# Four chained layers on one core: layer 3's opening set among layer 2's last steps

## The chip, the cores and the metric

The kernel runs on one core of a Trainium2 chip. A core has five engines: TensorE (PE) multiplies matrices, VectorE (DVE) and ScalarE (ACT) work elementwise, GpSimd (POOL) does simple elementwise work and memory fills, SyncE (SP) issues transfers. Each runs its own instruction list in order and waits on counters (semaphores) that others raise. Data lie in SBUF, products land in PSUM, which has eight banks. The metric is the device time of one execution in microseconds.

## The reference, cut to what matters

```python
x: (16, 64, 16, 16) f32
x = layer 0: group norm, 1x1 convolution, a gated mixture of basis functions; added to x
x = layer 1: group norm, a state-space block with a 3x3 depthwise convolution; added to x
x = layer 2: group norm, attention of 8 heads over the 256 places of an image; added to x
x = layer 3: group norm, modulated deformable 3x3 convolution; added to x

# layer 3, for each image
n      = group_norm(x)
offset = conv3x3(n, off_w) + off_b            # 18 channels: dy and dx of 9 taps
mask   = sigmoid(conv3x3(n, mask_w) + mask_b) # 9 channels
for tap in 9:                                 # ky, kx
    py, px = row + ky - 1 + dy, col + kx - 1 + dx
    samp[tap] = bilinear(n, py, px) * mask[tap]     # zero outside the image
x += weight . samp + bias
```

The opening norm of each layer is over pairs of channels of one image. Bilinear sampling is done without gathering: the weight of source row r for position py is a "hat", max(0, 1 - |py - r|), and likewise for columns, so that a sample is a matrix product with (row hat x column hat) as weights.

## The kernel before

Two images lie on the 128 partitions (64 channels each), so there are 8 pairs and 4 groups of 4 images. `program` calls `layer0` to `layer3` in turn; each has a block of its own, between which all engines meet at a barrier.

**Layer 2** (L761 to L1109) is a software pipeline written out by hand. `ROWS` (L777) are steps v from -19 to 143, eight for each image (k = v % 8, c = v // 8), and every engine's list goes through them. At step v TensorE computes score tiles for the maxima of step v + 19 (`largest`, L1027), until v = 108; the score tile v (`scores`, L1038), until v = 127; and, at fixed k, the products of the context (`context`, L1058), its turning (`turn_context`, L1072, k = 5), turning back (`turn_back`, k = 0) and the projection (`project`, k = 3). VectorE takes maxima, divides the context (`normalize`, k = 5) and adds the result to x (`add`, L925, k = 3); ScalarE takes exponentials of every score tile. POOL splits the maxima in two halves, SP sends them (`send_maxima`, L828) into the stacks `q_st` that the scores read. The last 16 steps have no scores left, only the last images' contexts.

**Layer 3** (L1112 to L1568) first has an opening. The norm of all pairs (`GroupNorm`, L114) goes through three engines; VectorE writes the padded images `xpad` (L1300), three queues send them into `stack` (L1175); TensorE convolves offsets and masks for group 0 (`conv_offsets`, L1459: 24 products and 4 for the grid), ScalarE takes them out of PSUM (`take_offsets`, L1362). For chunk 0 (4 images) positions and masks are spread to all places by products (`spread_positions` L1468, `spread_masks` L1475), in thirds of three taps; for later chunks they go through DRAM (`load_positions`, `load_masks`). From each third come the hats (`take_distance`, `make_hat`), weighed by the mask (`weigh_hat`, L1189) and split into three bf16 parts (`take_first`, `take_rest`, `take_second`, `take_last`), on VectorE and ScalarE for chunk 0, on POOL and ScalarE for the others. SP copies the parts into `hats[b]`, b = 0 or 1 for the pair of the chunk (`send_hats`, L1230). In between, TensorE weighs pair 0 (`weigh`, L1482) and convolves groups 1 to 3.

Then comes the loop over 8 pairs n and 9 taps t (L1554), v = 9 n + t. At each tap TensorE spreads the row hats of v + 1 and the column hats of v + 2 (`spread_rows`, `spread_cols`), weighs one sixth of the next pair in taps 2 to 7, and adds the samples of v to `acc` (`samples`, L1513). VectorE multiplies row and column weights (L1335) and copies one half of the weighed images (L1311); ScalarE copies the column weights (`take_cols`) and the other half, and does one of the 12 `hat_steps` (L1416) of the next chunk at each tap: step h of the chunk at tap h of its two pairs. `spread_cols` waits for the hats in SBUF at the start of each pair (L1505); `take_first` (L1389) waits until the former chunk's hats have left `parts`.

## Time and profile before

| | |
|---|---|
| three timed runs | 524.96, 528.49, 530.88 us; median 528.49 |
| profiled execution | span 528.0 us, first to last instruction; the page gives no other time for it |
| busy in the span | PE 439.1 us (83%), weight loads 231.3, DVE 342.4 (65%), ACT 288.9 (55%), POOL 132.8 (25%) |
| layer 2, steps from the first score tile | about 218 to 348 us |
| layer 3's opening | 348 to 383.6 us |
| layer 3's loop | 383.6 to 522.8 us |

Busy means that an instruction was under way, not that the engine was at its peak. The chain of waits that ended last shows PE with 13% of the span, POOL 6%, DMA 5%, SP's queue 3%, ACT 3%, DVE 2%; PE's granted clock has two levels, 1.0 (2.4 GHz) and 0.5 (1.2 GHz), and a number between them is a mean over a stretch.

### The profile page before, as it was taken

The page shows a single profiled execution, that of the slowest core. Times are in us where ns is not written, and L with a number is a line of the kernel's source. Part 1 is how long each engine was busy: PE and PEld are TensorE (multiplying, and loading weights), DVE is VectorE, ACT ScalarE, POOL GpSimd, SP SyncE. Part 2 cuts the span into 40 slices and gives each one's busy share as a digit, 9 for nine tenths or more (in the row PEclk, how much of TensorE's full clock was granted, in tenths as well). Part 3 has the DMA queues.
Part 4 walks back from the last instruction along what each step waited for, and adds up shares of the span by engine and source line. Part 5 has one row for each costly group of instructions (what it writes and reads, how often), then busy time and mean ns, then how long its engine had stood idle before and what let it go on. Part 6 is the DMA issues. An engine that isn't in the chain of part 4 may idle for free. (4 is left out here: it accounts for less than half of the span.)

```text
span 528.0 us, 9368 instructions
## 1 busy us (share of the span) xinstructions
PE 439.1 (83%) x3406; PEld 231.3 (44%) x3406; DVE 342.4 (65%) x668; ACT 288.9 (55%) x511; POOL 132.8 (25%) x162
## 2 busy tenths in 40 slices
PE   0527768899999887679999999939898999999995
PEld 0216648555455664223333333324443454454442
DVE  4549876233344568978999996251654778777784
ACT  1279955131532437047878778722865578486441
POOL 4420004000000005744422212031364428065000
PEclk9956997999999988559999999957977999999999
DMA  5500000900000004952200000016390480933302
GB/s 142 164 0 1 0 0 1 197 1 1 0 1 0 1 0 107 279 175 67 73 27 3 3 2 4 0 47 160 100 226 15 89 181 2 217 55 68 67 2 79
DMA packets 20767, 33.79 MB, mean 64 GB/s; under 512 B 5657, under 2 KB 15497, under 8 KB 19957
## 3 DMA queue, kind: packets, MB, share of 16 engines
q1 hardware_dynamic: 16724, 23.70, 18.9%
q0 software_dynamic: 2176, 6.35, 4.3%
q10 hardware_dynamic: 1824, 3.19, 2.3%
q8 instruction: 26, 0.43, 0.4%
q14 instruction: 17, 0.13, 0.1%
HBM read 16.21 MB, written 4.64 MB: 39 GB/s over the span
## 5 line engine op out<-in xcount | busy, mean ns | idle before, releaser
L1335 DVE TENSOR_TENSOR L_s<-L_row_ps,L_cols 128x1024 f32<-128x1024 f32 x72 | 87.6, 1218 | 9.3 <-PE L_row_ps L1500 7.5
L910 DVE TENSOR_REDUCE L_mx<-L_ring 128x2 f32<-128x512 f32 x128 | 83.3, 686 | 12.4 <-PE L_ring L1034 11.8
L965 ACT ACTIVATE L_e<-L_ring 128x512 f32<-128x512 f32 x128 | 73.7, 597 | 21.4 <-PE L_ring L1047 19.3
L1523 PE MATMUL L_acc<-L_s,L_t_sb 128*64 128x256 f32 x576 | 81.6, 406 | 1.1 <-DVE L_s L1335 1.0
L1404 ACT ACTIVATE L_cols<-L_col_ps 128x512 f32<-128x512 f32 x72 | 42.8, 596 | 48.9 <-PE L_col_ps L1510 48.5
L1034 PE MATMUL L_ring<-stacks_k_st,stacks_q_st 64*128 64x256 bf16 x256 | 51.0, 301 | 7.0 <-DMA stacks_k_st<-L_k_parts 4.7
L1523 PEld LDWEIGHTS L_acc<-L_s,L_t_sb 128*64 128x64 f32 x576 | 36.0, 140 | 35.9 <-DVE L_s L1335 19.8
L1047 PE MATMUL L_ring<-stacks_q_st,stacks_k_st 64*128 64x256 bf16 x256 | 47.2, 282 | 1.2 <-DMA stacks_q_st<-L_m_parts 1.2
L1500 PE MATMUL L_row_ps<-L_hats,L_sel 48*128 48x512 bf16 x144 | 44.6, 392 | 0.0
L1067 PE MATMUL L_ctx_ps<-L_e,L_v_x 128*32 128x256 f32 x512 | 41.5, 398 | 0.0
L1311 DVE COPY L_t_sb<-L_acc 128x192 f32<-128x192 f32 x48 | 17.1, 357 | 31.4 <-PE L_acc L1491 31.4
L1034 PEld LDWEIGHTS L_ring<-stacks_k_st,stacks_q_st 64*128 64x128 bf16 x256 | 15.9, 98 | 43.8 <-DVE L_mx L910 24.2
L382 PE MATMUL L_y<-L_t,all_w_post 128*128 128x256 f32 x96 | 25.3, 418 | 11.5 <-DVE L_t L342 11.5
L1510 PE MATMUL L_col_ps<-L_hats,L_sel 48*128 48x512 bf16 x72 | 28.7, 400 | 7.0 <-DMA L_hats<-L_parts 5.0
L1491 PE MATMUL L_acc<-all_w_all,L_xn 64*128 64x192 f32 x96 | 26.8, 362 | 5.0 <-DVE L_t_sb L1311 2.7
L382 PEld LDWEIGHTS L_y<-L_t,all_w_post 128*128 128x128 f32 x96 | 19.4, 208 | 17.1 <-DVE L_t L342 14.2
L1491 PE MATMUL L_col_ps<-all_w_all,L_xn 64*128 64x192 f32 x96 | 26.7, 360 | 0.0
L853 POOL MEMSET L_v_x<- 128x1024 f32 x1 | 1.0, 951 | 101.7 <-POOLq L496 101.7
L1200 POOL TENSOR_TENSOR L_hat<-L_hat,L_mask 64x768 f32<-64x768 f32 x9 | 16.3, 1812 | 40.1 <-ACT L_hat L1382 40.1
L415 ACT ACTIVATE L_uu<-L_z,L_minus_mu,L_inv 128x256 f32 x48 | 24.4, 586 | 1.3 <-DVEq L314 1.3
L633 ACT ACTIVATE L_sq<-L_t_ps 128x1024 f32<-128x1024 f32 x4 | 4.1, 1024 | 34.9 <-PE L_t_ps L716 34.9
L656 PE MATMUL L_xs_ps<-L_stack,L_w_tap 128*128 128x512 f32 x48 | 22.7, 601 | 0.0
(270 smaller groups left out, 814.2 us busy)
## 6 DMA issues: line engine op xcount, KB each, us to landing
L_hats<-L_parts SPq DMA_DIRECT2D x28, 216.0 KB, 5.0
L_hat<-L_offsets SPq DMA_DIRECT2D x20, 192.0 KB, 4.7
L_mask<-L_offsets SPq DMA_DIRECT2D x10, 192.0 KB, 4.9
stacks_q_st<-L_q_parts SPq DMA_DIRECT2D x12, 128.0 KB, 3.9
stacks_k_st<-L_k_parts ACTq DMA_DIRECT2D x12, 128.0 KB, 4.8
stacks_q_st<-L_q_parts POOLq DMA_DIRECT2D x12, 128.0 KB, 2.7
stacks_k_st<-L_k_parts POOLq DMA_DIRECT2D x12, 128.0 KB, 2.9
L_stack<-L_xpad SPq DMA_DIRECT2D x7, 162.0 KB, 5.8
```

The lines of the kernel that those rows point to most:

```text
L382: mm = pe.matmul(y2[:, ds(k, 1), :], w_post[:], t[:, q, j:j + 1, :], start=False, stop=(j == NB - 1))
L910: dve.tensor_reduce(mx[:, n % 2, :, head], ring[:, place(step) % 3].rearrange("p (q s) -> p q s", q=2), AX.X, ALU.max).then_inc(max_read, 1)
L965: act.activation(e[:, k], ring[:, 3 + v % 3], ACT.Exp, scale=HD2 ** -0.5).then_inc(e_ready, 1)
L1034: mm = pe.matmul(ring[:, place(step) % 3, q * N:(q + 1) * N], rows_of(q_st, n, h, p)[:, q * P:(q + 1) * P], rows_of(k_st, n, h, p), start= ...
L1047: mm = pe.matmul(ring[:, 3 + v % 3, t * N:(t + 1) * N], rows_of(k_st, c, h, p)[:, t * P:(t + 1) * P], rows_of(q_st, c, h, p), start=True, ...
L1067: mm = pe.matmul(ctx_ps[32 * j:32 * j + 32, g * N:(g + 1) * N], v_x[:, c % 2, t, 4 * g + j, :], e[:, 4 * g + j, t * N:(t + 1) * N], start= ...
L1335: dve.tensor_tensor(s[:, q], row_ps[:, q], cols[:, t % 3:t % 3 + 1].broadcast_to([P, 2, 2 * N]), ALU.mult).then_inc(s_ready, 1)
L1404: act.activation(cols[:, v % 3], col_ps[:, c % 2], ACT.Copy).then_inc(col_read, 1)
L1491: mm = pe.matmul(out, xn[rows, b, k // 3 * P:(k // 3 + 1) * P], w_all[rows, k % 3 * TW:(k % 3 + 1) * TW], start=True, stop=True)
L1500: mm = pe.matmul(row_ps[:, v % 2, h], sel[0:3 * H, h], hats[0:3 * H, n % 2, :, t * N:(t + 1) * N], start=True, stop=True)
L1510: pe.matmul(col_ps[:, c % 2], sel[C:C + 3 * H, 2], hats[C:C + 3 * H, n % 2, :, t * N:(t + 1) * N], start=True, stop=True).then_inc(col_rea ...
L1523: mm = pe.matmul(acc[C * e:C * e + C, b, 0:N], t_sb[:, b, h, (KK * e + t) * C:(KK * e + t + 1) * C], s[:, q, h, e * N:(e + 1) * N], start= ...
```

## The change

Layer 3's opening gets a class of its own, `Opening`, whose methods are called from layer 2's step lists and then from layer 3. Its norm is done in two lots of four pairs; its buffers `parts`, `hats`, `s` and `cols` lie in layer 2's stacks, and the padded images stay in memory from layer 0 on (`Pads`), cleared once on POOL. In layer 2, lot 0's norm stands at steps 79 to 85, group 0's offsets at 109 to 115, chunk 0's first two thirds of hats at 116 to 134 with part of the last third, and group 1's offsets at 137 to 143. What is left for layer 3 is the end of the last third, lot 1's norm and pair 0's weighing. The offsets of groups 2 and 3 are convolved after taps (0, 8) and (1, 5) of the loop. Masks in layer 2 are made of exp and ln instead of the sigmoid table. The ScalarE hat steps of chunks 1 and 2 come two taps later. All transfers of layer 3 are issued by SP.

```diff
 # layer 2, SP
+for j in range(4):
+    send_maxima(NQ - 1, j)
+    if j < 2:
+        opening.send_group(sp, j)
+sp.wait_ge(s_ready, 8 * 12)
+sp.wait_ge(opening.parts_ready, 2)
+opening.send_hats(sp, 0, slice(0, 2 * opening.THIRD))
 # layer 2, POOL, after image n
+if n in (12, 13):
+    opening.pad_group(pool, x, n - 12)
+if n == 14:
+    opening.copy_selection(pool)
+    for p in range(2):
+        opening.normalize_pair(pool, x, p)
 # layer 2, VectorE, at the end of step v
+if v == 79:
+    dve.wait_ge(signals.x_stats, 3 * NP + 4)
+    opening.aggregate(dve, 0)
+if v == 83:
+    opening.variances(dve, 0, a_ps[:, P:P + 4])
+if v == 85:
+    opening.shifts(dve, 0)
+if v == 116:
+    opening.take_offsets(dve, 0, ring[:, 2, 0:N])
+if v in (118, 125):
+    opening.below_by_vector(dve, (v - 118) // 7, pos_ps)
+if v in (119, 126):
+    opening.hat_by_vector(dve, (v - 119) // 7, pos_ps)
+if v in (121, 128):
+    opening.weigh_hat(dve, (v - 121) // 7, mask_ps, True)
+if v == 122:
+    opening.take_first(dve, 0)
+if v == 123:
+    opening.take_rest(dve, 0)
+if v == 124:
+    opening.take_second(dve, 0)
+if v == 125:
+    opening.take_last(dve, 0)
+if v == 131:
+    opening.take_rest(dve, 1)
+if v == 133:
+    opening.take_last(dve, 1)
+if v == 134:
+    opening.weigh_hat(dve, 2, mask_ps, False)
 # layer 2, ScalarE, at the end of step v
+if v == 84:
+    opening.scales(act, 0, a_ps[:, P + 4:P + 8])
+if v == 116:
+    opening.take_masks(act, 0)
+if v == 129:
+    opening.first_by_scalar(act, 1)
+if v == 130:
+    opening.distance_by_scalar(act, 2, pos_ps)
+if v == 132:
+    opening.second_by_scalar(act, 1)
+if v == 131:
+    opening.hat_by_scalar(act, 2)
+if v == 143:
+    opening.offsets_by_scalar(act, 1, ring[:, 0, 0:N])
+    opening.take_masks(act, 1)
 # layer 2, TensorE, within step v
+if v == 83:
+    pe.wait_ge(ctx_copied, c - 1)
+    opening.means(pe, 0, a_ps[:, P:P + 4])
+if v == 84:
+    opening.spreads(pe, 0, a_ps[:, P + 4:P + 8])
+if 109 <= v < 116:
+    if v == 109:
+        pe.wait_ge(max_read, 126)
+    opening.convolve(pe, 0, ring[:, 2, 0:N], v - 109, v - 108)
+if v == 117:
+    pe.wait_ge(max_read, 8 * B)
+    pe.wait_ge(m_read, B)
+    opening.spread_positions(pe, 0, pos_ps)
+if v in (123, 130):
+    third = (v - 116) // 7
+    pe.wait_ge(opening.masked, third)
+    opening.spread_positions(pe, third, pos_ps)
+if v in (120, 127, 132):
+    third = (v - 120) // 6
+    pe.wait_ge(opening.dist_ready, third + 1)
+    if third < 2:
+        pe.wait_ge(opening.hat_ready, third + 1)
+    opening.spread_masks(pe, third, mask_ps)
+if v >= 137:
+    if v == 137:
+        pe.wait_ge(opening.dist_ready, 3)
+    opening.convolve(pe, 1, ring[:, 0, 0:N], v - 137, v - 136)
...
+class Opening:
...
+    def convolve(self, pe, g, out, first, last):
...
+        for k in range(first, last):
+            for j in range(4):
+                if k < 6:
+                    pe.matmul(out[32 * j:32 * j + 32], w_off[:, k, :], tap(self.stack, 4 * g + j, k), start=(k == 0), stop=False)
+                else:
+                    mm = pe.matmul(out[32 * j:32 * j + 32], w_grid[:], grid[:], start=False, stop=True)
...
+    def take_masks(self, act, g):
+        act.wait_ge(self.off_ready, g + 1)
+        act.activation(self.sig[:, g], self.off[:, g], ACT.Exp, scale=-1.0).then_inc(self.mask_own, 1)
+        act.wait_ge(self.mask_own, 2 * g + 1)
+        act.activation(self.sig[:, g], self.sig[:, g], ACT.Ln, bias=1.0).then_inc(self.mask_own, 1)
+        act.wait_ge(self.mask_own, 2 * g + 2)
+        act.activation(self.sig[:, g], self.sig[:, g], ACT.Exp, scale=-1.0).then_inc(self.sig_ready, 1)
...
+CONVOLVED = {(0, 8): 2, (1, 5): 3}
+MASKED = {(0, 8): (), (1, 0): (2,), (1, 7): (3,)}
 # layer 3, SP (all transfers of the layer)
+store_group(sp, 1)
+sp.wait_ge(stored[1], 32)
+load_positions(sp, 1, 0)
+load_masks(sp, 1, 0)
+sp.wait_ge(parts_ready, 3)
+sp.wait_ge(hats_in[0], 64)
+opening.send_hats(sp, 0, slice(2 * THIRD, TN))
+for g in (2, 3):
+    opening.send_group(sp, g)
+for j in (1, 2):
+    load_positions(sp, 1, j)
+    load_masks(sp, 1, j)
+opening.send_hats(sp, 1, slice(0, TN))
+store_group(sp, 2)
 # layer 3, VectorE, before the loop
+opening.aggregate(dve, 1)
+dve.wait_ge(first_ready, 2)
+for k in range(2):
+    take_first_image(0, k, k, first_ps[k])
+opening.variances(dve, 1, mean_ps)
+dve.wait_ge(first_ready, 4)
+for k in range(2, 4):
+    take_first_image(0, k, k, first_ps[k])
+opening.take_rest(dve, 2)
+for k in range(4, 6):
+    take_first_image(0, k, k, first_ps[k])
+opening.shifts(dve, 1)
+opening.take_last(dve, 2)
 # layer 3, ScalarE, in the loop
+                    late = 2 if n < 4 else 0
...
-                        h = KK * (n % 2) + t
-                        if n < NP - 2 and h < len(hat_steps):
+                        if (n, t) in CONVOLVED:
+                            g = CONVOLVED[n, t]
+                            opening.offsets_by_scalar(act, g, col_ps[:, turns.bank["conv", g], 0:N])
+                        if (n, t) == (0, 0):
+                            act.preload_act_table_set("sigmoid_and_others")
+                        h = KK * (n % 2) + t - late
+                        if n < NP - 2 and 0 <= h < len(hat_steps):
                             hat_step, j = hat_steps[h]
                             hat_step(n // 2 + 1, j)
 # layer 3, TensorE, in the loop
                         samples(n, n % 2, t)
+                        if (n, t) in CONVOLVED:
+                            g = CONVOLVED[n, t]
+                            bank_read(("conv", g))
+                            opening.convolve(pe, g, col_ps[:, turns.bank["conv", g], 0:N], 0, 7)
```

## Rows read from the trace of the kernel before

**Rows 1.** Table of stretches: us, busy us (instructions) of each engine, granted clock, DMA share, GB/s.

```profile
330.90:337.00 6.10, 5.77 (x58) 2.29 (x57) 1.09 (x4) 5.08 (x10) 0.20 (x1) 1.00 0.00 1
...
347.90:383.60 35.70, 27.19 (x282) 14.96 (x283) 15.90 (x43) 18.30 (x31) 12.69 (x20) 0.79 0.46 116
...
383.60:399.50 15.90, 13.87 (x84) 6.12 (x82) 9.54 (x11) 8.03 (x14) 7.13 (x9) 0.81 0.90 195
...
399.50:407.00 7.50, 6.84 (x30) 3.27 (x31) 2.98 (x4) 4.74 (x10) 4.17 (x3) 0.54 0.01 2
...
423.50:439.50 16.00, 16.00 (x127) 8.24 (x125) 12.92 (x17) 12.48 (x25) 5.96 (x4) 1.00 0.61 129
```

**Rows 2.** Timeline of the seam: start, us, engine, line, what; last: barrier passed.

```profile
328.87 0.39 PE L1047 MATMUL L_ring<-stacks_q_st,stacks_k_st 64*128 64x256 bf16 x2
...
329.18 0.64 PE L1067 MATMUL L_ctx_ps<-L_e,L_v_x 128*32 128x256 f32 x8
...
340.96 0.33 PE L1083 MATMUL L_a_ps<-all_ident,L_ctx_n 128*128 128x128 f32 x1
...
347.99 1.28 ACT L174 ACT_TABLE_LOAD   x1 [2.44 <-PEq L823]
```

**Rows 3.** Timeline of TensorE: positions, masks (not shown), positions, convolution, the next one.

```profile
364.76 1.56 PE L1472 MATMUL L_row_ps<-L_off,all_to_places 128*128 128x256 f32 x6
...
367.69 1.56 PE L1472 MATMUL L_row_ps<-L_off,all_to_places 128*128 128x256 f32 x6
...
370.67 2.80 PE L1463 MATMUL L_row_ps<-L_stack,all_w_off 128*32 128x256 f32 x48
...
373.71 2.77 PE L1463 MATMUL L_row_ps<-L_stack,all_w_off 128*32 128x256 f32 x48
```

**Rows 4.** Timeline of ScalarE and VectorE in the opening, and a group of the page.

```profile
364.60 0.47 ACT L1365 ACTIVATE L_sig<-L_row_ps,all_l_vec 128x256 f32<-128x256 f32 x1
...
368.16 0.68 DVE L1196 TENSOR_TENSOR L_hat<-L_hat,L_row_ps 64x512 f32<-64x512 f32 x1 [8.14 <-ACT L_hat L1382]
...
370.95 0.96 DVE L1208 TENSOR_TENSOR L_rest<-L_hat,L_parts 128x768 f32<-128x768 f32 x1 [1.78 <-ACT L_parts L1391]
...
L1311 DVE COPY L_t_sb<-L_acc 128x192 f32<-128x192 f32 x48 | 17.1, 357 | 31.4 <-PE L_acc L1491 31.4
```

**Rows 5.** Chain of waits: a transfer's issue, the landing of pair 1's hats; transfers by size.

```profile
383.07 0.59 SPq L1173
...
392.01 6.66 DMA L_hats<-L_parts
...
L_stack<-L_xpad SPq DMA_DIRECT2D x7, 162.0 KB, 5.8
```

**Rows 6.** Timeline of the loop: VectorE's first samples, then TensorE's taps.

```profile
383.64 2.36 DVE L1335 TENSOR_TENSOR L_s<-L_row_ps,L_cols 128x1024 f32<-128x1024 f32 x2 [1.31 <-ACT L_cols L1404]
...
400.16 0.60 PE L1510 MATMUL L_col_ps<-L_hats,L_sel 48*128 48x512 bf16 x1 [1.97 <-ACT L_cols L1404]
...
403.32 0.60 PE L1500 MATMUL L_row_ps<-L_hats,L_sel 48*128 48x512 bf16 x1
...
406.82 0.39 PE L1500 MATMUL L_row_ps<-L_hats,L_sel 48*128 48x512 bf16 x1
...
408.37 0.39 PE L1500 MATMUL L_row_ps<-L_hats,L_sel 48*128 48x512 bf16 x1
...
422.54 0.39 PE L1510 MATMUL L_col_ps<-L_hats,L_sel 48*128 48x512 bf16 x1 [1.08 <-DMA L_hats<-L_parts]
```

**Rows 7.** Chain of waits, and timeline of TensorE: chunk 2's third hat, its landing.

```profile
438.00 0.74 ACT L_hat L1382
...
455.81 0.39 PE L1510 MATMUL L_col_ps<-L_hats,L_sel 48*128 48x512 bf16 x1 [0.92 <-DMA L_hats<-L_parts]
```

**Rows 8.** Timeline of VectorE in layer 2: a cast alone, one beside POOL.

```profile
201.05 0.43 DVE L895 CAST L_parts<-L_e 128x512 bf16<-128x512 f32 x1
...
206.25 1.26 DVE L895 CAST L_parts<-L_e 128x512 bf16<-128x512 f32 x1
```

632 lines of the change are left out of this document (345 added, 287 removed).

## The prediction

> **What bounds the kernel now.** I read the table of stretches first, then the timeline of each engine around the seam between layers 2 and 3, then the chain of waits. In about steps 115 to 122 of layer 2 (330.9 to 337.0) TensorE is busy 5.77 of 6.10 us while VectorE does 1.09 us and POOL almost nothing; in layer 3's opening, 347.9 to 383.6, it is busy 27 of 35.7 us at a granted clock of 0.79; in a settled image pair of the sampling loop it is busy 16.00 of 16.00 us [rows 1]. So the seam costs 35.65 us from the barrier (347.99) to the first sample multiplication (383.64) [rows 2, 6], and the time is won only if the work put among layer 2's steps fits where TensorE is idle. It mostly doesn't: a score step takes 0.31 us (328.87 to 329.18) and a context step follows at once [rows 2]. TensorE is itself what bounds those steps; the idle engine there is VectorE. Only the last steps (128 to 143, from 340.96 to 347.7) have holes, because there each product waits for the one before.
>
> **The change, part by part.**
>
> *Norm of the first four pairs at steps 79 to 85.* Nine small VectorE operations and two small products. VectorE works beside a TensorE that never waits long, but the spread product waits in TensorE's order for four dependent VectorE steps. Between nothing (all hidden) and 1.5 us; I take 0.5, since the products themselves are tiny.
>
> *First offsets at steps 109 to 115.* Seven pieces of the convolution, 28 products. The same 28 took 3.04 us (370.67 to 373.71) at full clock [rows 3]. TensorE is full there, so all of it lengthens layer 2: **+3.0**.
>
> *Positions and masks at steps 117, 120, 123, 127.* One third of both took 2.93 us (364.76 to 367.69) [rows 3]. Two thirds: **+5.9**.
>
> *The wait before step 127's masks.* TensorE waits in its own order for `hat_ready`. VectorE has, since the first masks landed, to weigh the hat (0.68, then about 0.4 and 0.6 for the two smaller pieces), cast it, take the rest (0.96), cast again (0.65 each, by 0.43 for 512 columns), add an image and divide another (about 1.1), then do two operations over 768 columns out of PSUM with a subtraction of 0.96 between them [rows 4, 8]. Two PSUM multiplications of 1024 columns take 2.36 [rows 6], so 768 take about 0.9. With ten hand-overs of about 0.1 that is 8.9 us after the first masks' end, against 6.6 us of TensorE's own work (seven rows of 0.3 to 0.9, and 1.45 of positions) [rows 2, 3]. I take **+2.3**; between 0 and 5. Behind it in TensorE's order stand the contexts and everything of the tail.
>
> *The tail, steps 128 to 143.* Before, from 340.96 to the barrier at 347.99, 7.0 us [rows 2]. Now in this order: turning back and two context steps (1.4), a wait for the second weighing (0.3), positions (1.5), projection (0.6), the wait for ScalarE's distance (0.6), masks (1.45), turning image 15 (0.6), its division (0.9), turning back and two pieces of convolution (1.2), projection (0.6), the other pieces (2.1), ScalarE's offsets and three dependent operations for the mask (0.47 each, with gaps 2.1) [rows 3, 4]. With 0.3 for the barrier 13.6 us, so **+6.6**; between +3 (the holes swallow a third's products) and +9.
> Layer 2 thus ends at 347.99 + 0.5 + 3.0 + 5.9 + 2.3 + 6.6 = **366.3**.
>
> *Moved to POOL and SP.* Padding and the xn copies are POOL's at images 12 to 14, where it idles; two groups of stack transfers go between maxima, four instructions of 0.63 us each [rows 5], inside a lead of a whole image, about 7 us. Cost nothing; without that cover, two stalls of about 2 us.
>
> *What is left of the opening.* VectorE: aggregation 0.35, six copies of 0.36, five small operations with their hand-overs 1.2, the third's rest and last part 0.96 each [rows 4], and about 1.2 of waits for ScalarE and TensorE: 6.8 us, between 6 and 9. The first multiplication is at 373.1 instead of 383.64, 10.5 us earlier. The two-thirds hats were issued in layer 2's tail and are in by then.
>
> *The transfers after it.* This is what is late next. SP now issues, alone and in order: group 1's two stores and a wait for their landing (3.5 us), three loads (1.9), then waits for the third part (6.8), four hat transfers, eight stack transfers of groups 2 and 3 (of about 160 KB), six loads, and only then pair 1's four hat transfers: 22 times 0.63, so the last is issued at 6.8 + 14.0 = 20.8 us after the barrier and lands 5.0 to 6.7 later [rows 5]. The volume agrees: 3.6 MB at the 195 GB/s of the loop's first 16 us is 18 us [rows 1]. Pair 1's hats are in at 26.3 us, 392.6; before they came at 398.67 (392.01 and 6.66) [rows 5]. Tap 7 of pair 0 cannot begin before. Before it began at 403.32 [rows 6]; now at 392.7: **-10.6**. Both have a stop of about 2 us ahead of it, and before, the clock then was 0.54 over 7.5 us [rows 1]. Its price was two taps of about 3.5 (403.32 to 406.82) instead of 1.9, one of them before 403.32 [rows 6]. I take the same cost after tap 7 as before; between 1.6 cheaper and 3.3 dearer.
>
> *Offsets of groups 2 and 3 between taps.* A tap is TensorE's from end to end: 1.55 us without weighing (406.82 to 408.37) [rows 6], and (16.0 - 3 x 1.55) / 6 = 1.89 with it [rows 1]. Twice 3.04 [rows 3]: **+6.1**. VectorE has one tap in hand and covers none of it.
>
> *The hat steps two taps later.* They are tied to taps on ScalarE, and each chunk's hats must land before tap 7 of an odd pair. Chunk 1 before: TensorE stood 1.1 us until 422.54 [rows 6]. Chunk 2 before: ScalarE's third hat (438.00) began a chain over POOL, SP and the transfer that landed 17.8 us later, just before 455.81, and TensorE waited about 1 us for it [rows 7]. In the new chunk 1 that hat stands behind group 2's convolution, about 33.6 us after the barrier, so the chain ends at 51.4, where TensorE arrives at 48.7: 2.7 of waiting, **+1.6**; between 0 and 4. In the new chunk 2 the chain begins two weighed taps later (2 x 1.89) while TensorE arrives as before: **+3.8**; between 0 and that.
>
> **Sum.** -10.6 + 6.1 + 1.6 + 3.8 = +0.9 us. The page gives a span of 528.0 and no other time for that execution; it is 0.5 below the median of the three runs, 528.49 (524.96 to 530.88). So 528.49 + 0.9 = **529.4 us**: no change that can be told, 1% (5.3 us) being about what a measurement of this kernel tells from nothing.
>
> A third weighing: POOL pads groups 2 and 3 while VectorE forms the last part in the opening. The trace has such a pair: a cast of 512 columns takes 0.43 us alone and 1.26 beside POOL's subtraction [rows 8]. The Trainium skill, "SBUF — State Buffer", section Who interferes with whom, says that the two engines share one port pair, that a VectorE instruction with two SBUF inputs or in a two-port mode contends with POOL, and that whoever comes second waits the whole instruction. By that rule the third part would be late by one POOL operation, at most about 0.8 us, and the sum 530.2; by the row of 0.96 for the same subtraction it is 529.4.
>
> **Rivals.**
> *Faster: the waits are not there.* If VectorE is ahead at step 127 (-2.3), the tail grows by 3 only (-3.6) and the full clock holds after the stop (-1.6), and the late hat steps cost half (-1.9), the time is 520.0. For it: the tail's TensorE is free for half its length; my hand-overs are generous. Against it: each of the four is a sum of measured operations. Chance 0.27.
> *Slower: the clock falls in layer 2's tail.* The place is step 127, the first wait of more than 2 us in a stretch that ran at 1.00 throughout. After such a stop at 398.2 to 400.16 the granted clock was near its lower level of 1.2 GHz (0.54 in that stretch), and a row product took 0.60 us instead of 0.39 [rows 1, 6]. If it falls there, it decides the case: positions, masks and the second convolution, 1.45 + 1.45 + 3.04 and the turns between, take about 6 us more, and the opening's twelve weighings and first taps 2 more: 537. It needs the wait to reach about 2 us, which my sum has just over that line. For it: before, the seam itself ran at 0.79 [rows 1]. Against it: here there are 1.4 us products between the waits. Chance 0.21.
> The Trainium skill, "TensorE: Matmul & The Clock Gate", section HAM oscillation, says that waits between bursts throttle the array again, so that the next burst starts slow; this trace agrees at 400 us.
> *Slower: the maxima.* If a stack group's 0.65 MB holds image 14's maxima back, two stalls of 2 us: 533.3 and, with any of the above, over the line. Chance 0.05.
> *The change doesn't do what it says*, the work staying in a row because a semaphore holds it to the old order: about 529 to 535. Chance 0.02.
>
> **Chances.** The forecast's own case has 0.45, with its own range 524 to 534. Faster by over 1% (under 523.2): the first rival, 0.27. Within 1%: 0.46. Slower (over 533.8): 0.21 + 0.05 and a little: 0.27. The range of 8 in 10 runs from the faster rival's value to just beyond the clock's: 519 to 538.
>
> **What would show it.** Right: the barrier to layer 3 at about 366 and the first row-and-column multiplication at about 373; TensorE's steps 109 to 127 longer by some 11 us, with one wait of 2 to 3 us before a mask product; pair 1's hats landing 26 us after the barrier; two taps of 5 us with the convolutions in them; waits of about 2.7 and 5 us before tap 7 of pairs 1 and 3, and of about 1 before that of pair 5 as before. Wrong: a barrier before 362 or after 371; a granted clock of 0.5 in layer 2's last steps; no longer wait before tap 7 of pair 3, which would mean that the hats are not tied as I say.

## The result: slower by 2.3%, and where the profile after shows it

The changed kernel took 539.15 us (median of four runs, 537.00 to 542.91); beside it on the same chip the kernel before took 527.53 us (four runs, 524.96 to 530.88). The ratio is 1.0229, 95% interval 1.0171 to 1.0287. Ratios here come from runs side by side without the slower executions (over 1.5% above the fastest of their kernel), medians and ranges from all of them, so that the quotient of two medians can differ from the ratio by up to 0.4%. The forecast was 529.4 with a range of 519 to 538, and "within 1%" as the likeliest of three. It was wrong. The profiled execution of after took 539.36 us, its span is 537.6: 9.6 more than the span of before. The account below is made of spans.

The page of the kernel after: span, busy time, and the granted clock in 40 slices of 13.4 us.

```profile
span 537.6 us, 9381 instructions
PE 445.5 (83%) x3422; PEld 234.1 (44%) x3422; DVE 345.4 (64%) x670; ACT 284.2 (53%) x510; POOL 123.1 (23%) x147
PEclk9857988999999997579999999995859999799899
```

TensorE's busy time grew by 6.4 us with 16 more matrix instructions recorded, so most of that is slower instructions, not more of them. In the clock row the digits below 9 late in the span are slices 28 and 29 from the left counted from zero (376 to 403 us), 34 (457 to 470) and 37 (497 to 511), beside the opening's own (27). The table of stretches shows the first of them closer (us, busy us of each engine, granted clock, DMA share, GB/s):

```profile
358.00:365.00 7.00, 4.21 (x61) 2.18 (x62) 2.90 (x8) 2.00 (x5) 0.00 (x0) 0.96 0.28 89
365.00:374.00 9.00, 7.84 (x35) 5.19 (x35) 5.31 (x18) 4.58 (x12) 2.70 (x4) 0.50 0.28 95
...
384.00:394.00 10.00, 7.12 (x38) 2.79 (x34) 4.01 (x5) 3.24 (x7) 2.63 (x2) 0.72 0.85 174
394.00:404.00 10.00, 9.63 (x77) 4.36 (x80) 2.71 (x3) 2.97 (x5) 1.64 (x1) 0.60 0.00 0
```

Layer 2's barrier was passed at 364.8 us (SP's first instruction behind it; forecast 366.3) and the first sample multiplication came at 373.36 (forecast 373.1; before 383.64, [rows 6]). Up to there the change does what it should: it wins 10.3 us. Then the loop gives back 19.9. VectorE multiplies samples once per tap, so the start of that instruction is a clock on every tap, and the timelines of the two kernels give this table (starts of the sample multiplication, us):

| from tap (pair, tap) | to | before | after | more | forecast |
|---|---|---|---|---|---|
| (0,0) at 383.64, 373.36 | (0,8) | 21.66 | 22.40 | +0.7 | -0.1 |
| (0,8) | (1,3) | 7.41 | 13.48 | +6.1 | +3.05 |
| (1,3) | (1,7) | 7.51 | 11.14 | +3.6 | +3.05 |
| (1,7) | (2,1) | 6.22 | 7.36 | +1.1 | +1.6 |
| (3,7) | (4,2) | 7.60 | 14.12 | +6.5 | +3.8 |
| (5,7) | (6,1) | 6.18 | 7.94 | +1.8 | 0 |

All other taps are equal to 0.02 us. The sum (before rounding) is +19.9, less 10.3 is +9.6, the whole difference of the spans. The three rows that were missed most are the three in which a stop of TensorE is followed by slow instructions. First, the timeline around the end of pair 0 (start, us, engine, line, what, and in brackets the idle time before and who ended it):

```profile
387.09 0.94 ACT L1634 ACTIVATE L3o_shared<-L3o_shared,all_l_vec 128x768 f32<-128x768 f32 x1 [3.02 <-DMA L_mask<-L_masks]
...
388.56 0.60 PE L1754 MATMUL L_col_ps<-stacks_q_st,L3o_sel 48*128 48x512 bf16 x1 [1.63 <-ACT stacks_q_st L1661]
...
394.37 0.60 PE L1754 MATMUL L_col_ps<-stacks_q_st,L3o_sel 48*128 48x512 bf16 x1 [1.62 <-DMA stacks_q_st<-stacks_k_st]
...
400.32 3.64 PE L1331 MATMUL L_col_ps<-stacks_stack,all_w_off 128*32 128x256 f32 x48
...
404.52 0.47 ACT L1345 ACTIVATE L3o_off<-L_col_ps,all_l_vec 128x256 f32<-128x256 f32 x1 [5.37 <-PE L_col_ps L1333]
404.89 0.83 ACT L1640 ACTIVATE L3o_shared<-L3o_shared 128x768 f32<-128x768 f32 x1
```

ScalarE stands 3.0 us for chunk 1's loads, with TensorE behind it; then TensorE stands for pair 1's hats until 394.4. A column product takes 0.60 us where it takes 0.39 at full clock, and group 2's convolution takes 3.64 us against 2.80 [rows 3]: the granted clock is 0.50 from 400.3 to 402.0 and 0.99 behind that. ScalarE waited 5.37 us for it, and its hat (404.89) stood behind. SP's queue says why both transfers were late:

```profile
373.22 2.49 SPq L1439 DMA_DIRECT2D stacks_q_st<-stacks_k_st  x4
375.76 0.65 SPq L1310 DMA_DIRECT2D stacks_stack<-stacks_xpad  x1
...
380.38 0.61 SPq L1311 DMA_DIRECT2D stacks_stack<-stacks_xpad  x1
381.03 1.25 SPq L1509 DMA_DIRECT2D L3o_shared<-L_offsets  x2
...
385.57 2.77 SPq L1439 DMA_DIRECT2D stacks_q_st<-stacks_k_st  x4
```

Eight stack transfers that nobody needs before tap 8 stand ahead of the loads (tap 4 to 7) and of the hats (tap 7). Second, TensorE's timeline before tap 7 of pair 3 and behind it, with the stretch it lies in:

```profile
455.59 0.60 PE L1743 MATMUL L_row_ps<-stacks_q_st,L3o_sel 48*128 48x512 bf16 x2
...
460.94 0.61 PE L1754 MATMUL L_col_ps<-stacks_q_st,L3o_sel 48*128 48x512 bf16 x1 [4.75 <-DMA stacks_q_st<-stacks_k_st]
...
462.12 1.97 PE L1767 MATMUL L_acc<-stacks_k_st,L_t_sb 128*64 128x256 f32 x8
...
464.03 0.60 PE L1743 MATMUL L_row_ps<-stacks_q_st,L3o_sel 48*128 48x512 bf16 x1
```
```profile
460.00:466.00 6.00, 5.06 (x22) 2.27 (x24) 2.39 (x3) 1.80 (x4) 0.00 (x0) 0.51 1.04 264
466.00:472.00 6.00, 6.00 (x45) 2.54 (x43) 4.14 (x6) 4.30 (x8) 1.48 (x1) 0.92 0.89 165
```

The stop was 0.92 us before [rows 7] and is 4.75 now: 3.83 more, the forecast to 0.03. What was not forecast is the line at 462.12: the samples of a tap take 1.97 us instead of 1.08, two taps run at the lower clock (1.2 GHz), and 2.7 us more are gone. In four experiments with this stop left as it is, (3,7) to (4,2) took 12.9 to 13.2 us instead of 14.1, so the part behind the stop is 1.4 to 2.7 us, by the execution.

The other rows vary by execution too. The row from (1,7) has a stop of 2.19 us behind which the clock stayed up:

```profile
423.85 0.39 PE L1754 MATMUL L_col_ps<-stacks_q_st,L3o_sel 48*128 48x512 bf16 x1 [2.19 <-DMA stacks_q_st<-stacks_k_st]
...
424.49 1.08 PE L1767 MATMUL L_acc<-stacks_k_st,L_t_sb 128*64 128x256 f32 x8
```

In five experiments that leave this place alone (chunk 2 on time, step 127, both fills, the convolution two taps later) the stop is 2.0 to 2.3 us, the clock fell at it each time, and the row took 8.7 to 10.4 us instead of 7.4. The row from (0,8) took 11.4 to 12.5 us in four experiments that leave it alone, instead of 13.5. In the one whose loop is wholly unchanged (step 127) the loop from first to last sample multiplication took 154.8 us, here 156.2, before 136.3: the whole differs by 1.4 us, the row from (3,7) alone by 1.3 and the one from (1,7) by 1.6 the other way.

### The profile page after: what moved, and what is told of

The parts are those of the page before. It is cut to its first block and busy times, and to the rows that moved or that the text cites. A ratio compares the mean times of both kernels' runs of the same rounds, so it can differ in the third digit from the quotient of the medians.

```text
span 537.6 us, 9381 instructions
## 1 busy us (share of the span) xinstructions
PE 445.5 (83%) x3422; PEld 234.1 (44%) x3422; DVE 345.4 (64%) x670; ACT 284.2 (53%) x510; POOL 123.1 (23%) x147
## 3 DMA queue, kind: packets, MB, share of 16 engines
q1 hardware_dynamic: 18608, 25.70, 19.3%
## 5 line engine op out<-in xcount | busy, mean ns | idle before, releaser
L1609 DVE TENSOR_TENSOR stacks_k_st<-L_row_ps,stacks_q_st 128x1024 f32<-128x1024 f32 x72 | 87.6, 1218 | 17.5 <-PE L_row_ps L1743 17.0
L932 DVE TENSOR_REDUCE L_mx<-L_ring 128x2 f32<-128x512 f32 x128 | 83.4, 686 | 10.9 <-PE L_ring L1101 10.2
L1767 PE MATMUL L_acc<-stacks_k_st,L_t_sb 128*64 128x256 f32 x576 | 84.6, 418 | 0.9 <-DVE stacks_k_st L1609 0.8
L1661 ACT ACTIVATE stacks_q_st<-L_col_ps 128x512 f32<-128x512 f32 x72 | 42.9, 596 | 55.0 <-PE L_col_ps L1754 54.8
L1767 PEld LDWEIGHTS L_acc<-stacks_k_st,L_t_sb 128*64 128x64 f32 x576 | 37.1, 144 | 38.5 <-DVE stacks_k_st L1609 18.1
L1743 PE MATMUL L_row_ps<-stacks_q_st,L3o_sel 48*128 48x512 bf16 x144 | 46.2, 404 | 0.1
L1754 PE MATMUL L_col_ps<-stacks_q_st,L3o_sel 48*128 48x512 bf16 x72 | 30.0, 416 | 12.6 <-DMA stacks_q_st<-stacks_k_st 9.9
L383 PE MATMUL L_y<-L_t,all_w_post 128*128 128x256 f32 x96 | 25.0, 415 | 11.7 <-DVE L_t L343 11.7
L1557 POOL TENSOR_TENSOR L3o_shared<-L3o_shared,L_mask 64x768 f32<-64x768 f32 x9 | 16.3, 1816 | 65.1 <-ACT L3o_shared L1640 65.1
L1734 PE MATMUL L_col_ps<-all_w_all,L3o_xn 64*128 64x192 f32 x92 | 25.4, 363 | 0.0
L1734 PE MATMUL L_acc<-all_w_all,L3o_xn 64*128 64x192 f32 x88 | 23.9, 356 | 0.6 <-ACT stacks_q_st L1661 0.3
L663 PE MATMUL L_xs_ps<-stacks_stack,L_w_tap 128*128 128x512 f32 x48 | 22.7, 601 | 0.0
```

Source lines behind the costliest of these rows:

```text
L383: mm = pe.matmul(y2[:, ds(k, 1), :], w_post[:], t[:, q, j:j + 1, :], start=False, stop=(j == NB - 1))
L932: dve.tensor_reduce(mx[:, n % 2, :, head], ring[:, place(step) % 3].rearrange("p (q s) -> p q s", q=2), AX.X, ALU.max).then_inc(max_read, 1)
L1609: dve.tensor_tensor(s[:, q], row_ps[:, q], cols[:, t % 3:t % 3 + 1].broadcast_to([P, 2, 2 * N]), ALU.mult).then_inc(s_ready, 1)
L1661: act.activation(cols[:, v % 3], col_ps[:, turns.bank["cols", v]], ACT.Copy).then_inc(col_read, 1)
L1734: mm = pe.matmul(out[e], xn[rows, b, k // 3 * P:(k // 3 + 1) * P], w_all[rows, k % 3 * TW:(k % 3 + 1) * TW], start=True, stop=True)
L1743: mm = pe.matmul(row_ps[:, v % 2, h], sel[0:3 * H, h], hats[0:3 * H, n % 2, :, t * N:(t + 1) * N], start=True, stop=True)
```

## The experiments

Each time is compared with runs of the kernel before that were taken beside it on the same chip. "At (p,t)" is tap t of pair p.

### Chunk 2's hat steps on time

```diff
-                    late = 2 if n < 4 else 0
+                    late = 2 if n < 2 else 0
```

> Only chunk 2's hat steps go back to their old taps (two taps earlier); chunk 1's stay late. Theory A (the delay of the hat steps is what makes the stop before tap 7 of pair 3, and the stop is what drops the clock): the stop falls from 4.75 us to about 1, no tap after it runs at the lower clock, and between the sample multiplications of (3,7) and (3,8) lie 3.1 to 3.6 us instead of 7.4. That gives back 6.5 us: about 532.7 us, ratio to the kernel before 1.010. Theory B (the chain is late because POOL and SP still work on chunk 1 and on group 3's stores): the chain ends as late as now, the stop stays over 4 us, ratio 1.02.

534.08 us (531.71 to 541.50), ratio 1.0116, interval 1.0060 to 1.0171: about 1.1% under the change as it is. Theory A holds as to the time. The profiled execution is itself the longest of the five (541.5 us), so its clock is not typical of them. In it the stop before tap 7 of pair 3 is 2.15 us, and the clock then stays low until past 470 us.

```profile
460.99 0.39 PE L1754 MATMUL L_col_ps<-stacks_q_st,L3o_sel 48*128 48x512 bf16 x1 [2.15 <-DMA stacks_q_st<-stacks_k_st]
```
```profile
460.00:466.00 6.00, 5.01 (x27) 1.93 (x27) 2.71 (x3) 1.90 (x4) 0.00 (x0) 0.72 1.04 251
466.00:472.00 6.00, 6.00 (x27) 2.32 (x25) 2.84 (x3) 2.75 (x4) 1.11 (x1) 0.50 0.70 124
```

The stop is not back at 0.92 us, and that is no matter of this execution: in the profiles of the three later experiments with the same steps on time and the same loads behind the hats it is 2.17 or 2.18 us. The two taps are 2.6 of the 3.83 us. The other 1.2 lie in the transfers: from SP's first issue of the hats to TensorE's use of them it is 6.9 us in the kernel before and 8.15 here (452.84 to 460.99):

```profile
448.89 2.66 SPq L1236 DMA_DIRECT2D L_hats<-L_parts  x4
```
```profile
452.84 2.67 SPq L1439 DMA_DIRECT2D stacks_q_st<-stacks_k_st  x4
```

### Pair 1's hats ahead of the stacks

```diff
                 opening.send_hats(sp, 0, slice(2 * THIRD, TN))
-                for g in (2, 3):
-                    opening.send_group(sp, g)
-                for j in (1, 2):
-                    load_positions(sp, 1, j)
-                    load_masks(sp, 1, j)
+                load_positions(sp, 1, 1)
+                load_masks(sp, 1, 1)
                 opening.send_hats(sp, 1, slice(0, TN))
+                load_positions(sp, 1, 2)
+                load_masks(sp, 1, 2)
+                for g in (2, 3):
+                    opening.send_group(sp, g)
```

> SP's order after the third hats is changed alone: loads of chunk 1's second third, pair 1's four hats, loads of the last third, and only then the eight stack transfers of groups 2 and 3. Theory A (SP's order of issue sets both stops of pair 0: ScalarE's 3.0 us wait for the loads at 387.1 and TensorE's wait for pair 1's hats until 394.4): pair 1's hats are in at about 386, TensorE never stops 1.5 us in pair 0, the granted clock stays at 1.00, taps 7 and 8 take 1.9 instead of 5.6 and 2.8 us, and group 2's convolution 3.1 instead of 6.4 less 1.55. Some 3 + 2 + 1.9 + 0.9 = 7 to 9 us less: about 531, ratio 1.007; the later waits (1,7) and (3,7) may take 1 to 2 of it back, since chunk 1's chain then meets a TensorE that arrives sooner. Theory B (the transfers are bound by volume, not by order): the hats land at 391 or later, and the stacks then hold up the convolution; ratio 1.02.

531.47 us (531.00 to 532.86), ratio 1.0092, interval 1.0061 to 1.0123. Theory A. The clock is full after pair 0's first taps, and from (0,6) to (1,1) it takes 9.8 us instead of 19.3:

```profile
384.00:394.00 10.00, 9.97 (x80) 5.36 (x79) 8.31 (x11) 8.30 (x16) 5.28 (x3) 1.00 1.04 216
394.00:404.00 10.00, 9.65 (x104) 4.61 (x104) 4.83 (x7) 6.32 (x12) 5.15 (x4) 1.00 0.10 32
```

Some comes back at once, but not by the way that was expected. TensorE arrives 7 us sooner and (1,7) to (2,1) takes 10.2 us instead of 7.4, yet the stop in it is 2.28 us against 2.19: the hats moved along with the taps. What is new is the lower clock behind the stop, which the profile of the kernel after does not have there:

```profile
416.91 0.60 PE L1755 MATMUL L_col_ps<-stacks_q_st,L3o_sel 48*128 48x512 bf16 x1 [2.28 <-DMA stacks_q_st<-stacks_k_st]
...
418.08 1.97 PE L1768 MATMUL L_acc<-stacks_k_st,L_t_sb 128*64 128x256 f32 x8
```

From (0,8) to (1,3), with the same convolution and the full clock, it takes 10.4 us; the forecast had 10.5 (7.41 and 3.05), the profile after 13.5.

### Both together

The two edits above.

> Both edits together. If the two losses are separate places, the gains add: 539.2 - 6.5 - 7.5 = 525, ratio 0.996, within half a per cent of the kernel before. If the clock or one chain links them, the sum is smaller: ratio 1.005 to 1.01.

527.54 us (522.03 to 534.62, ten runs), ratio 0.9966, interval 0.9924 to 1.0009. The gains add: 1.0116 and 1.0092 are 0.0113 and 0.0137 under 1.0229, and 0.9966 is 0.0263 under it. The runs scatter over 12.6 us, with stops of 2.2 us left in the profile.

### Without the late convolutions

This kernel leaves out the 24 products over the stacks in each of the two convolutions; the last argument lets the four grid products start the sum.

```diff
...
-                            opening.convolve(pe, g, col_ps[...], 0, 7)
+                            opening.convolve(pe, g, col_ps[...], 6, 7, True)
```

> Left out: the 24 products over the stacks in the convolutions of groups 2 and 3; only the four grid products of each remain, so the offsets of images 8 to 15 are wrong. All waits, stores, loads and transfers stay. Theory A (the convolutions cost their own time on TensorE, more for group 2 since it runs at the lower clock): 3.6 us at the lower clock and 2.6 at full clock go, 6 us in all, and what hangs behind group 2 (ScalarE's third hat of chunk 1 at 404.9) comes 3.6 us earlier too, so no wait before tap 7 of pair 1 grows: 532 to 533 us, ratio 1.010. Theory B (the hat chain, not TensorE, sets the end of each two pairs): TensorE arrives earlier and waits longer before (1,7) and (3,7), and less than 3 us is gained, ratio 1.017.

536.90 us (534.93 to 540.52), ratio 1.0215, interval 1.0160 to 1.0269; span 533.1, 4.5 under the change. So B is nearer: (0,8) to (1,7) takes 5.6 us less, but (1,7) to (2,1) takes 11.7 us instead of 7.4. Of these 4.3 us, 1.6 are the stop (3.77 us instead of 2.19), because the hats of chunk 1 do not come sooner by as much; the other 2.7 are slow taps, since here the clock fell at that stop (0.50 from 418.8 to 425.6) and in the profile after it did not. How much of the convolutions' own time a chain of hats takes back, one execution of each does not tell.

### Everything early

```diff
-                load_positions(sp, 1, 0)
-                load_masks(sp, 1, 0)
+                for j in range(3):
+                    load_positions(sp, 1, j)
+                    load_masks(sp, 1, j)
                 sp.wait_ge(parts_ready, 3)
                 sp.wait_ge(hats_in[0], 64)
                 opening.send_hats(sp, 0, slice(2 * THIRD, TN))
+                opening.send_hats(sp, 1, slice(0, TN))
                 for g in (2, 3):
                     opening.send_group(sp, g)
-                for j in (1, 2):
-                    load_positions(sp, 1, j)
-                    load_masks(sp, 1, j)
-                opening.send_hats(sp, 1, slice(0, TN))
...
-                    late = 2 if n < 4 else 0
+                    late = 1 if n < 2 else 0
```

> SP issues all of chunk 1's loads ahead of its wait for the third part (it idles from 368.9 to 373.2 there), then the third hats, pair 1's hats, and the stack transfers last; chunk 1's hat steps stand one tap late instead of two, chunk 2's on time. Theory A (what is left in the run with both first edits is chunk 1's chain: 3.0 us of waiting before tap 7 of pair 1 and 1.7 of slow taps behind it): the wait goes, (1,7) to (1,8) takes 1.9 us instead of 4.5, and the whole is 4 us under that run: 523.5 us, ratio to the kernel before 0.989. Theory B (POOL's nine operations of a chunk, about 15.5 us, set the end whatever the taps): the wait shrinks by less than 1 us and the ratio stays 0.996.

524.96 us (522.96 to 529.07, ten runs), ratio 0.9972, interval 0.9936 to 1.0007. Between A and B: (1,7) to (1,8) takes 2.9 us (4.5 with both edits, 1.9 without a wait), and (1,7) to (2,1) 5.8 instead of 9.0; of these 3.2 us, 1.6 are the stop (0.66 us instead of 2.25) and the rest is the clock, which fell at the longer one. The median is 2.6 lower than with both edits, the ratio is not: against ten scattered runs the difference can't be told. The stop before tap 7 of pair 3 is 2.18 us, and the clock fell behind it (0.50 from 448.9 to 452.3).

### Step 127 of layer 2

```diff
 # VectorE
-                    if v == 125:
+                    if v == 126:
                         opening.take_last(dve, 0)
 # TensorE
-                    if v in (120, 127, 132):
+                    if v in (120, 132):
...
+                    if v == 129:
+                        pe.wait_ge(opening.hat_ready, 2)
+                        opening.spread_masks(pe, 1, mask_ps)
```

> Only layer 2's step 127 is changed: VectorE takes the first third's last part after the second third's hat instead of before it (0.93 us), and TensorE's second mask products stand at step 129, behind one context step (0.42 us). Theory A (the 2.32 us stop and the lower clock in the masks behind it, 2.79 us instead of 1.5, come from this order): the stop falls to about 1.0, the masks take 1.5, the layer's barrier comes 2 to 2.6 us earlier, about 537, ratio 1.018. Theory B (the tail is bound by another chain, VectorE to ScalarE to TensorE for the last third and images 14 and 15): the barrier moves by less than 0.7 us, ratio 1.022.

536.63 us (534.21 to 538.71), ratio 1.0193, interval 1.0118 to 1.0269: in the direction of A, but the intervals overlap, so the traces must decide. The stop and the masks in the kernel after, and its stretch:

```profile
347.06 1.01 DVE L1382 SCALAR_TENSOR_TENSOR L3o_shared<-L_ring,all_l_vec,L3o_shared 128x768 f32<-128x768 f32 x1
...
348.16 2.79 PE L1369 MATMUL L_ring<-L3o_sig,all_to_places 128*64 128x256 f32 x6 [2.32 <-issue]
```
```profile
345.80:351.00 5.20, 2.88 (x11) 1.32 (x14) 2.26 (x3) 0.60 (x1) 0.00 (x0) 0.67 0.00 0
```

and in the experiment:

```profile
349.10 1.02 DVE L1385 SCALAR_TENSOR_TENSOR L3o_shared<-L_ring,all_l_vec,L3o_shared 128x768 f32<-128x768 f32 x1
...
350.17 1.51 PE L1372 MATMUL L_ring<-L3o_sig,all_to_places 128*64 128x256 f32 x6
```
```profile
345.80:351.00 5.20, 5.06 (x45) 2.24 (x44) 5.05 (x9) 2.45 (x5) 0.00 (x0) 1.00 0.00 0
```

No stop, masks of 1.51 us, clock 1.00. That execution came to this hat 2.0 us later than the other (349.10 against 347.06), and to the first sample multiplication 0.5 earlier (372.89 against 373.36): the stretch between is 2.5 us shorter. That is no measure of the edit alone, since the edit moves this hat, and since the clock need not fall at this stop. In three other experiments that keep it (both together, without the late convolutions, filled with all rows) it did not:

```profile
351.42 1.48 PE L1369 MATMUL L_ring<-L3o_sig,all_to_places 128*64 128x256 f32 x6 [2.32 <-issue]
```

(This is from both together.) From the first third's hat (336.83 us) to SP's first instruction behind the barrier it is 28.0 us in the profile after, 26.7 in those three and 25.9 here: 0.8 us for the stop, and 1.3 for the clock where it falls. A is right that both come from this order, but for the clock not in every execution.

### The stop filled with products over 48 rows

```diff
+                    if v == 4 * KK:
+                        bank_read(("cols", v))
+                        for _ in range(20):
+                            pe.matmul(col_ps[:, bank], sel[C:C + 3 * H, 2], hats[C:C + 3 * H, 1, :, 0:N], start=True, stop=True)
                     if t == 0 and n:
                         pe.wait_ge(hats_in[n % 2], ...)
```

> Twenty products of 512 columns that nobody reads fill TensorE's 4.75 us stop before tap 7 of pair 3; nothing else changes, and the hats land as late as before. Theory A (an idle TensorE is what drops the clock): no lower clock after it, (4,0) and (4,1) take 1.27 and 1.65 us instead of 2.77 and 2.43, the third of the loss behind the stop (2.3 us) comes back and the stop itself stays: (3,7) to (3,8) 6.9 to 7.4 us; the time 537, ratio 1.018. Theory B (the clock falls there for another reason, the transfers or the chip's load): no change, or fill that pushes the tap later: ratio 1.023 to 1.026.

538.65 us (536.41 to 541.95), ratio 1.0243, interval 1.0160 to 1.0325. Theory A fails as stated. TensorE was busy to within 0.86 us of the hats, at a granted clock of 1.00 (458 to 463 us), and the first samples behind the stop ran at the lower one:

```profile
458.30 4.26 PE L1752 MATMUL L_col_ps<-stacks_q_st,L3o_sel 48*128 48x512 bf16 x19
...
463.42 0.39 PE L1758 MATMUL L_col_ps<-stacks_q_st,L3o_sel 48*128 48x512 bf16 x1 [0.86 <-DMA stacks_q_st<-stacks_k_st]
...
464.06 1.98 PE L1771 MATMUL L_acc<-stacks_k_st,L_t_sb 128*64 128x256 f32 x8
```
```profile
463.00:468.00 5.00, 4.58 (x24) 1.93 (x24) 2.45 (x3) 1.74 (x4) 0.00 (x0) 0.66 1.04 265
```

(3,7) to (4,2) took 12.95 us, as with the stop left alone (12.9 to 13.2). That left two readings: the fill was too weak, or the transfers (265 GB/s in the same stretch) are what it follows.

### The stop filled with products over all rows

```diff
+                        for _ in range(9):
+                            pe.matmul(col_ps[:, bank, 0:N], w_all[:, 0:P], w_all[:, P:P + N], start=True, stop=True)
```

> The stop before tap 7 of pair 3 is filled again, now by nine fp32 products over all 128 rows (4.4 us) instead of twenty bf16 products over 48 rows, after which the clock fell all the same. Theory A (what counts is how much of the array works, not that something runs): the clock stays up, (4,0) and (4,1) take 1.27 and 1.65 us, 1.7 to 2.3 us less than with the change as it is: 537, ratio 1.019. Theory B (the fall comes with the burst of transfers or is set by what ran earlier): the clock falls again, ratio 1.023.

535.81 us (534.76 to 538.21), ratio 1.0170, interval 1.0120 to 1.0220.

```profile
457.48 4.15 PE L1752 MATMUL L_col_ps<-all_w_all 128*128 128x256 f32 x18
...
462.29 0.39 PE L1758 MATMUL L_col_ps<-stacks_q_st,L3o_sel 48*128 48x512 bf16 x1 [0.66 <-DMA stacks_q_st<-stacks_k_st]
...
462.93 1.08 PE L1771 MATMUL L_acc<-stacks_k_st,L_t_sb 128*64 128x256 f32 x8
```
```profile
460.00:466.00 6.00, 5.34 (x35) 2.71 (x33) 2.71 (x3) 1.90 (x4) 0.00 (x0) 1.00 1.03 241
```

The same hats landing as late (6.96 us after their first issue, as in the profile after), the same transfers (241 GB/s), 0.66 us of idle time at the end for 0.86; but the samples take 1.08 us, (4,0) and (4,1) take 1.33 and 1.59 (2.77 and 2.44 in the profile after), and (3,7) to (4,2) 11.4 us: 2.7 less than in the profile after, 1.4 to 1.8 less than in the four other executions with this stop (the fill over 48 rows bought nothing). This speaks for Theory A: the clock fell in all five executions with this stop unfilled and in the one filled over 48 rows, and not in this one, under the same burst of transfers. It is not proven. It is one execution, and at the shorter stops of this kernel the clock falls in some executions and not in others; and the two fills differ in the type of the products (bf16, fp32) as well as in the rows. The medians (3.3 us under the change) point the same way with intervals that overlap.

### The two best edits together with step 127

The edits of "Everything early" and of "Step 127 of layer 2".

> The edits of e5_all_early and e6_step127 together. If both places are independent: 523.5 - 2.3 = 521 us, ratio 0.985, faster than both kernels. If the earlier barrier only makes the transfers meet TensorE sooner, no better than e5_all_early: 0.989.

521.34 us (519.09 to 521.84), ratio 0.9896, interval 0.9832 to 0.9960; span 519.9. Faster than both kernels: about 1% under the one before, 3.3% under the change. Here the stop before tap 7 of pair 3 is 2.17 us and the clock stayed up behind it (samples of 1.08 us):

```profile
447.50 0.39 PE L1755 MATMUL L_col_ps<-stacks_q_st,L3o_sel 48*128 48x512 bf16 x1 [2.17 <-DMA stacks_q_st<-stacks_k_st]
...
448.14 1.08 PE L1768 MATMUL L_acc<-stacks_k_st,L_t_sb 128*64 128x256 f32 x8
```

### The next chunk's loads behind the hats

On top of the previous experiment.

```diff
                             sp.wait_ge(stored[c + 1], 32)
+                            sp.wait_ge(hats_in[0], 64 * c + 128)
                             for j in range(3):
                                 load_positions(sp, c + 1, j)
```

> On top of e8_early_and_127, SP waits for the landing of the even pair's hats before it issues the next chunk's nine loads. Theory A (the 1.3 us by which those hats land later than in the kernel before, 8.1 against 6.8 us from first issue to landing, is the loads sharing the transfer engines): the hats land 5 to 6 us after the first issue and the stop before tap 7 of pair 3, 2.17 us, falls under 0.6: (3,7) to (3,8) takes 1.9 to 2.4 us instead of 4.4; the time 519, ratio to the kernel before 0.985. Theory B (the hats' own four transfers take that long by themselves, or the loads now come too late for ScalarE's steps at (4,1) to (4,3)): no gain, ratio 0.99 or above.

529.33 us (527.11 to 531.66, twelve runs), ratio 1.0044, interval 1.0018 to 1.0070: 1.5% slower than without the wait. Four hat transfers issued at 443.29 landed before 450.44, 7.1 us instead of 8.1 (1.0 of the 1.3 us that A spoke of), but the loads are not the whole reason: the kernel after has the same loads right behind these hats, and they landed in 7.0.

```profile
453.93 2.69 SPq L1439 DMA_DIRECT2D stacks_q_st<-stacks_k_st  x4
456.67 1.63 SPq L1509 DMA_DIRECT2D L3o_shared<-L_offsets  x2
```

What differs between the traces is one packet of 0.02 MB on the instruction queue (q8). Over the profiles of the kernel after and of all experiments, the hats of pairs 2 and 4 took 6.9 to 7.0 us from first issue to landing with the loads behind them and no such packet among them, 7.9 to 8.2 with both, and 6.9 to 7.5 with such a packet and no loads. No experiment changes that packet alone.

The odd pair's hats stand on SP behind those loads, and ScalarE's `take_first` waits for them:

```profile
443.29 2.69 SPq L1442 DMA_DIRECT2D stacks_q_st<-stacks_k_st  x4
450.44 0.39 PE L1756 MATMUL L_col_ps<-stacks_q_st,L3o_sel 48*128 48x512 bf16 x1 [1.27 <-DMA stacks_q_st<-stacks_k_st]
450.46 1.19 SPq L1512 DMA_DIRECT2D L3o_shared<-L_offsets  x2
```
```profile
ACT stacks_k_st L1650 <- DMA stacks_q_st<-stacks_k_st: 8.1, 2, 4.1
```

Two waits of ScalarE, 8.1 us in sum, make (2,7) and (4,7) take 5.0 and 5.2 us instead of 1.9, and behind each the clock fell and the next tap took 3.2 and 3.3 us. I had counted the loads' own slack and not the hats queued behind them.

### Group 2's convolution two taps later

```diff
-CONVOLVED = {(0, 8): 2, (1, 5): 3}
-MASKED = {(0, 8): (), (1, 0): (2,), (1, 7): (3,)}
+CONVOLVED = {(1, 1): 2, (1, 5): 3}
+MASKED = {(1, 1): (2,), (1, 7): (3,)}
```

> Only group 2's convolution and ScalarE's offsets and masks of it move two taps, from tap 8 of pair 0 to tap 1 of pair 1; nothing is left out. Theory A (the convolution ran at the lower clock because it followed the stop, and it held ScalarE's third hat of chunk 1 until 404.9): it takes 3.1 to 3.3 us on top of its tap instead of 4.9, the third hat comes 4 us earlier and the wait before tap 7 of pair 1 shrinks: 1.5 to 3 us less, 536.5 to 537.5, ratio 1.018. Theory B (the lower clock follows the convolution wherever it stands, or POOL's chain sets tap 7): ratio 1.023.

540.54 us (539.81 to 541.87), ratio 1.0264, interval 1.0218 to 1.0310. The convolution did run at full clock (2.80 us instead of 3.64), yet (0,8) to (1,3) took 12.6 us instead of 13.5: with the convolution gone, taps run at the lower clock in its place (2.57 us instead of 1.55 at (1,1)).

```profile
405.81 2.80 PE L1331 MATMUL L_col_ps<-stacks_stack,all_w_off 128*32 128x256 f32 x48
```

And 12.6 us is no gain at all beside the 11.4 to 12.5 of the four experiments that leave the convolution where it was; the profile after, with 13.5, is the highest of its kind. Theory A's size was wrong, and the time shows no gain.

The same edit on top of the loads behind the hats:

> e9_loads_after_hats and e11_offsets_at_1_1 together. With the stop of pair 0 gone, the convolution runs at full clock at either tap, and chunk 1's third hat is ahead of it at either: Theory A says no difference from e9_loads_after_hats within 1 us, ratio 0.985. If the convolution at tap 8 still costs a hand-over to ScalarE that a tap without weighing behind it would hide (the tap there took 4.83 instead of 1.55 and 3.04), it gains 0.3 to 1 us.

528.68 us (525.93 to 533.69, twelve runs), ratio 1.0039, interval 1.0003 to 1.0074: no difference from the loads behind the hats, as expected.

## Why the prediction was wrong

Right were: the wait before step 127's masks (2.32 us for 2.3); the late hat steps' own stop (4.75 us for "about 5", +3.83 for +3.8); and that a convolution between taps is paid in full at full clock (group 3: +3.6 for +3.05; group 2, in the experiment with the hats first, 10.4 us for 10.5). Two numbers came out right by luck. The first multiplication was at 373.4 for 373.1, but the barrier was 1.5 us early (364.8 for 366.3) and the remaining opening 1.7 us longer (8.5 us for 6.8). The row from (1,7) is +1.1 for +1.6, but only because the clock stayed up behind its stop in that one execution; in five others it fell there, for 1.3 to 3.0 us more. Pair 1's hats landed at 394.3 for 392.6, and (0,8) came about 1 us later than forecast.

**The step that failed** is the one that priced the stops: "I take the same cost after tap 7 as before", and, in the late hat steps, a stop with nothing behind it. The forecast's sum is 8.7 us below the spans' difference, and what lies behind the three stops carries 7.5 of it: 3.0 around group 2's convolution, 2.7 behind the stop of pair 3, 1.8 at that of pair 5. These are slow instructions seen in the trace, and what waits for them (samples of 1.97 us instead of 1.08, granted clock 0.50). For pair 3 the fill over all rows kept the late hats and the clock, and 1.4 to 2.7 us were back; it is one execution. For pair 0 it is shown that SP's order makes both stops and that the clock is full without them (7.7 us of the medians come back); behind (0,8) that is 3.1 us by the two profiles, and how much of the rest is clock and how much waiting the runs do not part. At pair 5 the stop is 1.30 us and the clock fell in the profile after; in ten of the twelve experiments it did not ((6,0) took 1.33 us instead of 2.70), in two it did. Ahead of pair 0's tap 7 there were two stops (1.63 and 1.62 us) where one was forecast; the first came of ScalarE's wait for chunk 1's loads, which the sum has not. So each of these sizes belongs to one execution, between nothing and 3 us a stop, and the step failed in that it put nothing on them beyond what the kernel before already paid.

The lower clock was in the prediction, but as a rival tied to one place, step 127. There it did fall (masks of 2.79 us, granted clock 0.67 from 345.8 to 351) and came back at once, at a price of 1.3 us instead of the 8 given; in nine executions with this stop it fell in six. That the rival's 537 us is near the measured 539 is luck. The same mechanism at tap 7 of pair 3, where I forecast a stop of 5 us, got no price at all, although the row at 400.16 [rows 6] was before me. Nor does a stop have to reach "about 2 us": 1.30 us was followed by the lower clock and 2.19 us was not, in one execution.

POOL's pads (371.30 to 374.16) beside VectorE's last part: it took 0.99 us, and 0.94 in layer 2 with POOL idle. The side forecast of 0.8 us more did not show; 0.05 did.

What was wrong with the change itself: its 10.3 us are real, and three small orders lose them. SP's eight stack transfers ahead of loads and hats (7.7 us by medians), chunk 2's hat steps two taps late (5.1), VectorE's last part ahead of the second hat (2.5 by medians with intervals that overlap; 0.8 to 2.1 up to the barrier by the traces). With all three mended, and chunk 1's steps one tap late instead of two, it is at 0.9896 of the kernel before.

Open: what makes the clock fall at a stop of about 2 us in one execution and not in another. At tap 7 of pair 3 with the steps on time, stops of 2.15 and 2.18 us were followed by the lower clock and two of 2.17 and 2.18 were not; in the profile after, 1.30 us was and 2.19 us was not. This may be why the runs of a kernel with such stops scatter (522.0 to 534.6), but only one run of each kernel has a profile, so it is not shown.

## What to carry to other kernels

When work is moved out of a seam, list for every queue what now stands ahead of each transfer that the next stage needs, and issue in the order of need: here that alone was 1.4%. Price a stop of TensorE as the stop plus a stretch at the lower clock behind it, 1.4 to 2.7 us on top of 4.75 here and nothing to 3 us on top of 1.3 to 2.3, and give it as a range, since it differs from execution to execution; behind the kernel before's stops of 0.92 and 1.08 us nothing slow followed. Before explaining a gain or a loss by an edit, look whether the clock fell in both profiles at the places that the edit leaves alone. A step put back "where it is free" is only free if the queue behind it is not needed sooner: one wait on SP that was right for nine loads cost 8 us through four transfers behind them.

## What the runs showed of the hardware that I had not expected

- Keeping TensorE busy was not the same as keeping its clock. 4.3 us of bf16 products over 48 rows in a stop left the granted clock at 1.00 while they ran and at the lower level right behind it (samples of 1.98 us); 4.2 us of fp32 products over 128 rows in the same stop left it up (1.08 us). One execution each, and which of type and rows counts is not parted.
- The same stop in the same code is followed by the lower clock in one execution and not in another: 2.32 us before step 127's masks, six of nine; 1.3 us before tap 7 of pair 5, three of twelve.
- Moving a convolution out of the stretch at the lower clock did not save its slowness: it took 2.80 us instead of 3.64, but taps ran slow instead, and (0,8) to (1,3) took 12.6 us where four executions with the convolution in its old place took 11.4 to 12.5.
- Four hat transfers took 6.9 to 7.0 us from first issue to landing with nine loads issued behind them, and 7.9 to 8.2 when a packet of the instruction queue fell among them as well. What places the packet there, and whether it is the cause, no run shows.
